# A fused attention, scan and experts layer: keys and values computed from rounded parts of the context, key rows dealt by transfers

## The reference, cut to what matters

```
x = x + cross_attention(layernorm(x), ctx)     # 16 heads of 16, 1601 keys
x = x + selective_scan(layernorm(x))           # 16 states, rank 128
x = x + experts(layernorm(x))                  # 64 experts, top 8, capacity

q = qdq(x) @ qdq(wq).T + bq
kv = ctx @ wkv.T + bkv;  k, v = split(kv)      # what the change is about
o = softmax(q k^T / 4) v;  out = qdq(o) @ qdq(wp).T + bp
```

## Time and profile before

| | us |
|---|---|
| median of 3 runs | 2230.54 |
| profiled execution, device time | 2231.84 |
| its span in the trace | 2230.1 |
| mean granted TensorE clock (share of 2.4 GHz) | 0.972 |
| PE busy | 2087.4 (94%) |
| DVE busy | 1631.8 (73%) |
| ACT busy | 1519.4 (68%) |
| POOL busy | 597.7 (27%) |
| keys, matmuls of L597 (4096 instructions) | 399.0 |
| values, matmuls of L607 (1664 instructions) | 406.1 |
| keys' copies on ACT, L800 (256) | 152.7 |
| values' copies on DVE, L983 (224) | 145.9 |

### The profile page before, as it was taken

One profiled execution on the slowest core, in us unless ns is written; L12 is line 12 of the kernel. 1 busy time (PEld: TensorE's weight loads), 2 busy tenths in 40 slices (PEclk: granted clock), 3 DMA queues, 4 the chain that ended last, 5 costly groups with the idle time before them and its releaser, 6 DMA issues. The chain is left out here.

```text
span 2230.1 us, 54255 instructions
## 1 busy us (share of the span) xinstructions
PE 2087.4 (94%) x20746; PEld 1431.6 (64%) x20746; DVE 1631.8 (73%) x3522; ACT 1519.4 (68%) x3140; POOL 597.7 (27%) x604
## 2 busy tenths in 40 slices
PE   7999999999999999999999999999998559989965
PEld 4666666666666666666666666666665448868854
DVE  4447777878787878687878787777778747767746
ACT  2667776767686868676767777777768237757753
POOL 0001030303030312122121213030303127767770
PEclk9999999999999999999999999999999569999988
DMA  6475762213232222222222222221201147666748
GB/s 214 172 264 213 263 215 102 98 48 101 63 92 74 73 74 73 75 76 74 72 79 67 83 75 87 77 93 53 99 16 60 63 132 222 211 223 210 220 131 339
DMA packets 114271, 277.26 MB, mean 124 GB/s; under 512 B 19851, under 2 KB 70711, under 8 KB 107872
## 3 DMA queue, kind: packets, MB, share of 16 engines
q1 hardware_dynamic: 95584, 239.10, 32.7%
q0 software_dynamic: 18432, 34.69, 4.4%
HBM read 165.40 MB, written 108.27 MB: 123 GB/s over the span
## 5 line engine op out<-in xcount | busy, mean ns | idle before, releaser
L989 DVE TENSOR_REDUCE sb_negmax<-S 128x1 f32<-128x1604 f32 x256 | 467.7, 1827 | 145.6 <-PE S L622 139.7
L808 ACT ACTIVATE sb_probsT<-W 128x384 f32<-128x384 f32 (+1 forms) x1024 | 476.1, 516 | 90.7 <-PE W L632 86.5
L816 ACT ACTIVATE sb_probs<-S,sb_negmax 128x1604 f32<-128x1604 f32 x256 | 409.3, 1599 | 113.1 <-DVE sb_negmax L989 113.0
L632 PEld LDWEIGHTS W<-sb_ident,sb_probs 128*128 128x128 f32 (+1 forms) x3328 | 365.4, 139 | 185.8 <-ACT sb_K L800 133.3
L632 PE MATMUL W<-sb_ident,sb_probs 128*128 128x128 f32 (+1 forms) x3328 | 464.4, 278 | 6.5 <-ACT sb_probsT L808 2.5
L607 PE MATMUL W<-sb_wkv_in,sb_ctx 128*128 128x256 f32 (+1 forms) x1664 | 406.1, 386 | 14.3 <-ACT sb_probsT L808 12.4
L597 PE MATMUL W<-sb_ctx,sb_wkv_in 128*32 128x401 f32 x4096 | 399.0, 503 | 1.5 <-DMA sb_ctx<-ctxT 1.5
L800 ACT ACTIVATE sb_K<-W,sb_pair_cols 128x401 f32<-128x401 f32 x256 | 152.7, 596 | 279.9 <-PE W L597 279.8
L607 PEld LDWEIGHTS W<-sb_wkv_in,sb_ctx 128*128 128x128 f32 (+1 forms) x1664 | 293.4, 187 | 74.2 <-ACT sb_probsT L808 38.2
L1369 POOL DMA_INDIRECT y_scratch<-sb_ys,sb_places x256 | 254.0, 992 | 109.1 <-issue 74.4
L622 PE MATMUL S<-sb_K,sb_Q 32*128 32x400 f32 (+1 forms) x2048 | 244.3, 546 | 7.3 <-ACT sb_probs L816 6.1
(11 more groups left out here) (197 smaller groups left out, 2813.4 us busy)
## 6 DMA issues: line engine op xcount, KB each, us to landing
sb_ctx<-ctxT SPq DMA_DIRECT2D x32, 1604.0 KB, 7.6
xe_scratch<-sb_none SPq DMA_DIRECT2D x32, 1088.0 KB, 12.2
sb_xg<-xe_scratch SPq DMA_DIRECT2D x64, 544.0 KB, 4.1
sb_BC<-bc_scratch SPq DMA_DIRECT2D x32, 1024.0 KB, 6.2
sb_Q<-sb_q_own SPq DMA_DIRECT2D x128, 128.0 KB, 4.1
y_scratch<-sb_none SPq DMA_DIRECT2D x16, 1024.0 KB, 12.0
sb_rows<-y_scratch SPq DMA_DIRECT2D x16, 1024.0 KB, 8.1
sb_wgu<-wgu SPq DMA_DIRECT2D x64, 192.0 KB
```

The lines of the kernel that those rows point to most:

```text
L632: ins = pe.transpose(W[0:keys_in(t), at * P:(at + 1) * P], probs[n % 2][:, t * P:t * P + keys_in(t)], ident[:])
L808: act.activation(probsT[k][n % (k + 1)][:, 0:wide], ring[bank_of("T", G, k)][:, 0:wide], ACT.Copy)\
L816: act.activation(probs[n % 2][:].rearrange("p (c k) -> p c k", c=QUADS), scores_of, ACT.Exp, bias=negmax[:, slot:slot + 1], accum_out=den[ ...
L989: dve.tensor_reduce(negmax[:, slot:slot + 1], scores_of, AX.XY, ALU.max, negate=True).then_inc(max_done, 1)
```

## The change

Keys and values are computed as three products of rounded parts in float32r (hi x hi, lo x hi, hi x lo), as the experts already are. The weights are parted once at the start. The context is parted quarter by quarter: ScalarE copies 128 partitions x 2 x 402 elements to `ctx_hi`, VectorE subtracts into `ctx_lo`. The second batch of a pair is parted in slots 1 to 4, the first batch of the next pair in slots 7, 8, 10 and 11; the quarters are loaded again in the slots behind (2 to 5, and 8, 9, 11, 12). There is one `ctx` tile, loaded in quarters, instead of two.

A key job now computes one quarter of the columns for 128 features (four strips), with 128 x 128 weights and 402 columns, six slots ahead instead of four. ScalarE copies it to `K_f`, and four transfers per strip on SyncE's queue (`deal_keys`) lay its 32 features out into one of four `K` tiles, two slots before its scores; the scores wait for these transfers instead of ScalarE's copy. Columns per quarter become 402 (the last has 395).

Values are computed in slots 2 to 8 and 10 to 15 and, the last unit, slot 0; slots 1 and 9 have none. The queries' jobs move from slot 8 to slot 9, the second of them behind the keys. The partial sums of the first three scan units are no longer put off to the end of the slot.

```diff
-NO_VALUES = (0, 8)
+NO_VALUES = ()
+LEAD = 6
+OF = 4
+PART_AT = {1: (1, 0), 2: (1, 1), 3: (1, 2), 4: (1, 3), 7: (2, 0), 8: (2, 1), 10: (2, 2), 11: (2, 3)}
+LOAD_AT = {2: (2, 0), 3: (2, 1), 4: (2, 2), 5: (2, 3), 8: (3, 0), 9: (3, 1), 11: (3, 2), 12: (3, 3)}
-       (8, 0): ["XQ"], (8, 1): ["Q"], (10, 0): ["O0"],
+       (9, 0): ["XQ"], (9, 2): ["Q"], (10, 0): ["O0"],
-SUMMED_LATE = (0, 1, 2)
+SUMMED_LATE = ()
...
             def k_mm(n):
-                b, g, s = step_of(n)
+                batch, g, c = n // (2 * QUADS), n // QUADS % DT, n % QUADS
                 W = take("K", n)
-                pe.wait_ge(ctx_in[b], 16 * (n // SLOTS + 1))
...
-                for k in range(DT):
-                    for c in range(QUADS):
-                        ins = pe.matmul(W[32 * c:32 * c + 32, 0:CK], wkv_in[:, k, w0:w0 + 32],
-                                        ctx_t[b][:, k, c * CK:(c + 1) * CK], start=(k == 0), stop=(k == DT - 1))
+                pe.wait_ge(ctx_lo_up, batch * QUADS + c + 1)
+                products = [(w, x, k) for w, x in ((wkv_hi, ctx_hi), (wkv_lo, ctx_hi), (wkv_hi, ctx_lo)) for k in range(DT)]
+                for at, (w, x, k) in enumerate(products):
+                    ins = pe.matmul(W[:, 0:CK], w[:, k, g * P:(g + 1) * P], x[:, k, c * CK:(c + 1) * CK],
+                                    start=(at == 0), stop=(at == len(products) - 1))
...
             def v_mm(pair, b, unit):
-                    for k in range(DT):
-                        ins = pe.matmul(W[0:keys_in(t), n * D:(n + 1) * D], ctx_t[b][:, k, t * P:t * P + keys_in(t)],
-                                        wkv_in[:, k, D:2 * D], start=(k == 0), stop=(k == DT - 1))
+                    for at, (x, w, k) in enumerate(products):
+                        ins = pe.matmul(W[0:keys_in(t), n * D:(n + 1) * D], x[:, k, t * P:t * P + keys_in(t)],
+                                        w[:, k, D:2 * D], start=(at == 0), stop=(at == len(products) - 1))
...
+            def deal_keys(n):
+                four, s = divmod(n, STRIPS)
+                sp.wait_ge(ring_free["act"], free_at("K", four * QUADS + QUADS - 1))
+                after(sp, s_done, n - OF + 1)
+                for c in range(QUADS):
+                    sp.dma_start(K[n % OF][32 * c:32 * c + 32, :], K_f[four % 2][32 * s:32 * s + 32, c, :]).then_inc(k_in[n % OF], 16)
...
+            def part_ctx(batch, c):
+                act.wait_ge(ctx_in[c], 16 * (batch + 1))
+                if batch > 0:
+                    act.wait_ge(ring_full, full_at("K", (batch - 1) * 2 * QUADS + QUADS + c))
+                act.activation(ctx_hi[:, :, own], ctx_t[:, :, own], ACT.Copy).then_inc(ctx_hi_up, 1)
...
+            def part_low(batch, c):
+                dve.wait_ge(ctx_hi_up, batch * QUADS + c + 1)
+                dve.tensor_tensor(ctx_lo[:, :, own], ctx_t[:, :, own], ctx_hi[:, :, own].bitcast(F32), ALU.subtract).then_inc(ctx_lo_up, 1)
...
             def scores(n):
-                pe.wait_ge(ring_free["act"], free_at("K", n))
+                pe.wait_ge(k_in[n % OF], 16 * QUADS * (n // OF + 1))
...
             def load_ctx(batch, c):
+                after(sp, ctx_lo_up, (batch - 1) * QUADS + c + 1 if batch > 0 else 0)
```

More of the change, by code:

```diff
@@ L91, in values_at @@
     i, slot = divmod(G, SLOTS)
[L92 to L95, removed]
+    if 2 <= slot <= 8 and i < PAIRS:
+        return i, 1, slot - 2
+    if slot >= 10 and i + 1 < PAIRS:
+        return i + 1, 0, slot - 10
+    if slot == 0 and 0 < i < PAIRS:
+        return i, 0, len(V_UNITS) - 1
     return None
@@ L157, in held_by, with part_at @@
     return JOBS[NUMBER[job] - BANKS] if NUMBER[job] >= BANKS else None
+def part_at(G, at):
+    i, slot = divmod(G, SLOTS)
+    if slot not in at:
+        return None
+    ahead, c = at[slot]
+    return (2 * i + ahead, c) if 2 * i + ahead < BATCHES else None
 def multiplied_at(n, t):
@@ L245, in mixer_phase @@
         neg_half = sb("neg_half", [P, 1])
-        K = sb("K", [P, STRIPS, CK])
+        K_f = [sb(f"K_f{n}", [P, QUADS, CK]) for n in range(2)]
+        K = [sb(f"K{n}", [P, CK]) for n in range(OF)]
         V = [sb(f"V{n}", [P, KT, D]) for n in range(2)]
@@ L319, in mixer_phase @@
         w_mm = sem("w_mm")
-        ctx_in = [sem(f"ctx_in{n}") for n in range(2)]
+        ctx_in = [sem(f"ctx_in{n}") for n in range(QUADS)]
+        wkv_hi_up = sem("wkv_hi_up")
+        wkv_lo_up = sem("wkv_lo_up")
+        ctx_hi_up = sem("ctx_hi_up")
+        ctx_lo_up = sem("ctx_lo_up")
+        k_in = [sem(f"k_in{n}") for n in range(OF)]
         x_in = sem("x_in")
@@ L837, in _ @@
             act.wait_ge(kv_in, 16 * len(kv_loads))
-            for n in range(STRIPS):
+            act.activation(wkv_hi[:], wkv_in[:], ACT.Copy).then_inc(wkv_hi_up, 1)
+            for c in range(QUADS):
+                part_ctx(0, c)
+            for n in range(LEAD):
                 k_up(n)
@@ L914, in bank @@
                 return ring[bank_of(*job)]
[L917 to L918 removed]
+            dve.memset(S[:, 512 * (QUADS - 1) + CK_LAST:512 * (QUADS - 1) + CK], LOWEST).then_inc(lowest, 1)
             link_w = Chain(dve, dve_w, 0, 24)
@@ L1189, in _ @@
             dve.wait_ge(wq_in, 16)
-            for k in range(DT):
-                round_w(wq_rows, k)
+            round_w(wq_rows, 0)
+            dve.wait_ge(kv_in, 16 * len(kv_loads))
+            dve.wait_ge(wkv_hi_up, 1)
+            dve.tensor_tensor(wkv_lo[:], wkv_in[:], wkv_hi[:].bitcast(F32), ALU.subtract).then_inc(wkv_lo_up, 1)
+            part_low(0, 0)
+            round_w(wq_rows, 1)
+            part_low(0, 1)
             norm_q(0, q_link)
@@ L1194, in _ @@
             turned_wq()
-            dve.wait_ge(kv_in, 16 * len(kv_loads))
+            part_low(0, 2)
+            part_low(0, 3)
             for name, n in START:
@@ L1226, in _ @@
                         norm_o(job[1])
-                if slot == 8 and nxt:
+                if slot == 9 and nxt:
                     x_up(i + 1)
@@ L1246, in _ @@
                     route_link = route_begin(i - 2)
-                if slot == 8 and nxt:
+                if part_at(G, PART_AT):
+                    part_low(*part_at(G, PART_AT))
+                if slot == 9 and nxt:
                     q_out(i + 1)
```

87 lines of the change are left out of this document (51 added, 36 removed).

## The result

The changed kernel takes 2217.01 us (median of 4 runs, 2215.43 to 2217.85), the kernel before 2231.4 beside it. The ratio is 0.9935, 95% interval 0.9923 to 0.9947: faster by 14 us (0.65%), where 65 were forecast. The direction was right and the size was not; 2217 lies just above the range of 2100 to 2215.

A forecast was written before the change was run, and what follows sets the result against it. TensorE sets the slot; 9.7 us a pair leaves it, VectorE's waits and the port leave 3.6 won. Pair 0 9.5, pair 1 6, thirteen 46.8, last 4, less 1: 65.3, so 2165 us, range 2100 to 2215.

The forecast's parts named there:

- What leaves TensorE: TensorE's key and value products: cheaper by 9.7 us per pair together, so TensorE alone would need 97.1.
- the key term: TensorE's key jobs: 6 x 0.183 = 1.10 us instead of 1.46, 0.36 less per slot, 5.8 per pair.
- The waits: Steady pair: VectorE's lateness, through the ring banks, and the port make it 103.2 us, against 97.1 for TensorE alone.
- slots 10-0: Last stretch of a pair: VectorE's 41.1 us plus 2.0 of waits that stay, 43.1, 0.7 less than now.
- Slots 6-9: Third stretch of a pair: TensorE's 24.3 us plus 0.8 for parts and the xqT wait, 25.1, 1.5 less.
- The port: VectorE meeting POOL at the SBUF port, one to three times a pair: 1.0 to 3.1 us, taken as 1.2.
- Signs that failed: Steady pair: VectorE over 88% busy, keys waiting for values' copy in slots 10 to 12, slots 1-2 and 6-9 shortened most.
- deals hidden: Key-row transfers on SP: first strip of four ready 12 us before its scores, hidden by 5 us.
- a start that cost nothing: Before the first scores: two more keys and first parts cost more than cheaper values give back, 1 us.
- weights loaded beside the products: TensorE's weight loads stay hidden; the rival, loads in the open, about +1.1 us in 240 slots, 2495, had 0.02.
- 1-2 and 3-5: First two stretches of a pair: slots 1-2 take 13.2 us, 1.5 less; slots 3-5 take 20.6, 1.1 less.
- The second rival: Steady pair: three port meetings and VectorE's parts in slots 10-11 passed on whole, 105.5 us, 2198 to 2225; chance 0.19.

The follow-up runs named there:

- e12: e9 with both engines' partings of every batch but the first cut to 2 of 402 columns (context not rounded anew): 2155.7 us, one run.
- e1: Changed kernel with POOL multiplying the scan input of units 4 to 7 ahead of its scatters, not behind: 2194.4 us, ratio 0.9836.
- e9: Changed kernel with the three edits of e1, e4 and e5 together, nothing left out: 2178.67 us, ratio 0.9763.
- e3: Changed kernel with ScalarE's and VectorE's partings of every batch but the first cut to 2 of 402 columns: 2176.79 us, ratio 0.9756.
- e4: Changed kernel with the one-tile unit of values put back in slots 6 and 14: 2202.9 us, one run.
- e5: Changed kernel with the part of slot 8 moved to slot 9, behind the queries' copies, its load one slot later: 2199.11 us, one run.
- e2: Changed kernel with VectorE's subtraction alone cut to 2 of 402 columns for every batch but the first: 2178.22 us, one run.
- e8: Changed kernel with one of the four transfers of each key deal from the fifth strip on: 2219.53 us, one run.
- e6: Changed kernel with the sums of scan units 0 to 2 put off again, as before the change: 2216.24 us, one run.

## Why the prediction was off, step by step

- **"What leaves TensorE", 9.7 a pair: this is the step that failed.** It priced the products and left what stands beside them at nothing; the runs show 5.1 in place of 9.7. The distances between products were right, 0.18 and 0.12. But a job is not its distances times their number: keys took 1.30 and not 1.10, values 1.51 and not 1.44, the product with V 0.11 more, the transposes 0.08 less. That is 0.35 a slot, and in slot 5 next to nothing. Summed over the 16 slots of pair 8 from start to start, e12 against before: keys 2.9 less (5.8 forecast), values 3.4 less (3.9), the product with V 1.8 more and the transposes 0.5 less (both forecast unchanged), all else the same. So the key term was booked at twice its size, and a cost of 1.8 beside it at nothing. Measured, the pace is 101.7 (e12), 4.6 above my 97.1. Pair 0, which had VectorE free, shows it by itself: 5.1 instead of 9.5, or 6.4 at the same granted clock of 0.98, in e1's trace (95.3 against 101.7), whose pair 0 has the work of after. Why the ends of a job cost more than its middle, no run shows.
- **The waits, 6.1 a pair on top of TensorE's 97.1: 4.6 on top of 101.7.** After less e9 is 2.9 (three places of order), e9 less e12 is 1.65 (the parts). The split depends on the way taken: by e3 the parts are 2.9, and then 1.7 are left to the order. As amounts they were forecast not badly; on the right floor they eat up the whole gain. Of slots 10-0 I said that VectorE sets them, with 43.1; e12 needs 42.9 there at TensorE's own pace, so most of that time was TensorE's.
- **Slots 6-9, forecast 25.1, measured 27.75: the place that I misread.** The change starts values a slot later, so the one-tile unit left slot 6, where the projections for the scan need the room. I counted its smaller savings and not its place (e4: 0.7 in slots 6 and 7). In slot 9 I named the wait for the xqT copy but priced it in a sum of 0.8 with two others; with the queries moved there it is 1.0 alone (e5).
- **The port, 1.2 a pair: measured 1.6.** I named the mechanism and its cause (queries in slot 9 push POOL's work into a scan), and took one small meeting. It was one scan a pair, 1.63 longer, in the slot that already had values and a part. The row that I took the price from the earlier trace rows has one SBUF input; the scan has two. The parts themselves met POOL in slots 10 and 11 and did not grow: 0.99.
- **Signs that failed:** slots 6-9 were to be shortened most and got longer by 1.2; VectorE was to be busier than 88% of a steady pair and was busy for 87%, since the pair was longer than forecast; the keys' wait for the copy of values was named for slots 10 to 12 and is there once, in slot 11's keys.
- **Clock:** the forecast had no term for it. In this trace the stretches at a granted clock of 0.50 cost 1.4 us each in pairs 6, 10 and 14, 4 us in all.
- **Right:** parts of 0.99 on VectorE and 0.88 on ScalarE (0.92 forecast); VectorE's 92.7 us a pair (91.6 forecast); ScalarE's parts hidden (e2 against e3); deals hidden (e8); a start that cost nothing (first scores at 33.81 against 34.02 us, 1 us forecast); weights loaded beside the products (key products start 0.18 apart, each with a load of 0.19 of its own); slots 10-0 worse than 1-2 and 3-5.
- The second rival, VectorE pays all, 2198 to 2225 with 0.19, held the time, but by luck: with one port meeting instead of three, and only because TensorE had gained half of what I had booked.

Between the gain forecast (65) and the gain measured (14) lie 51 us. e9 gives back 38 of them by order (2.9 in each of thirteen steady pairs), and at 2178.7 it beats both kernels.

## What to carry to other kernels

Price a job by the distance from its first instruction to the first of the next job, in a row where it stands among the jobs it will stand among; distances inside a run leave out its ends, and over 16 slots and 16 pairs those were nearly half of the expected gain. When work moves a slot, list what each other thing in that slot had been placed there for. Where a faster engine hands a slot to the next one, 1 to 1.6 us on the wrong side of one wait, once a pair, cost some 17 to 22 us here, so try the order of the late engine before judging the change.

## What I had not expected of the hardware

- A `tensor_tensor_scan` of 512 elements with two SBUF inputs took 2.86 us instead of 1.23 beside one POOL multiplication of 1.31 that by its start came 0.46 after it, and 2.10 beside one that came 0.28 before it (e6). All 25 slowed scans of the two traces end 1.09 after POOL's multiplication, so nearly all of a scan's 1.23 lies behind it. In one more (304.35, slot 10 of pair 2) the multiplication came 0.73 after the scan; there the scan took 1.22 and POOL 1.57. The other way round, the subtraction of slot 10 began at 947.23 and took its 0.99, and POOL's multiplication, from 947.57 on, took 1.78. The Trainium skill (SBUF — State Buffer, SBUF: two separate sides) says that who starts first has the ports for the whole instruction. The subtraction agrees, and so do twelve of e6's thirteen slowed scans; the twelve of after do not by their start times. A scatter that runs on POOL when the scan begins doesn't explain it by itself: before has 27 scans that begin beside a scatter alone, and each took 1.23.
- A product of 402 columns had a distance of 0.18 in a job and about 0.24 at its two ends, next to float32 matmuls. Why, no run shows.
- The clears of the first 48 slots landed in 5.3 us instead of 12.2 with the context loaded in quarters instead of whole batches. Why was not tried.
